# A recurrent and attention block on one core: the norm's statistics by transposing, one projection per sequence, shifted sequences rounded by VectorE

## The reference, cut to what matters

```python
def shift_token(t):
    t1, t2 = jnp.split(t, 2, axis=-1)
    t2 = jnp.pad(t2, ((0, 0), (1, 0), (0, 0)))[:, :-1]
    return jnp.concatenate([t1, t2], axis=-1)

def _layer(x, wqkv, qs, ksc, wo, lg, lb, w1, b1, w2, b2):
    h = shift_token(x)
    qkv = h @ wqkv
    ...
    x = x + o @ wo
    h = shift_token(x)
    mu = h.mean(-1, keepdims=True)
    var = h.var(-1, keepdims=True)
    h = (h - mu) / jnp.sqrt(var + 1e-05) * lg + lb
    h = h @ w1 + b1
    a, g = jnp.split(h, 2, axis=-1)
    h = a * jax.nn.gelu(g, approximate=False)
    return x + h @ w2 + b2
```

## Time and profile before

| | |
|---|---|
| median of 3 runs | 1315.2 us (1311.35 to 1317.98) |
| the profiled execution | 1315.54 us, its span 1313.7 us |
| busy PE, DVE, ACT, POOL | 96%, 83%, 88%, 87% of the span |
| attention, layer 0 and layer 1 | about 20 to 535 us, about 680 to 1196 us of the span |

### The profile page before, as it was taken

The page is one execution under the profiler, slowest core; times in us unless marked ns, Lnnn a source line. Parts: engine busy times, 40 slices in busy tenths (PEclk is TensorE's granted clock), DMA queues, the critical chain, the costliest instruction groups (busy, mean ns, idle before and its releaser), DMA issues.

```text
span 1313.7 us, 38163 instructions
## 1 busy us (share of the span) xinstructions
PE 1264.7 (96%) x13793; PEld 1011.5 (77%) x13794; DVE 1088.4 (83%) x1883; ACT 1162.1 (88%) x3529; POOL 1147.3 (87%) x840
## 2 busy tenths in 40 slices
PE   7889999999999999899988999999999999999998
PEld 4777888888888887566657788888888888876776
DVE  6788888888888887599877888899988898983777
ACT  4778999999999998787768899999999999998886
POOL 4888999999999998399778999999999999984776
PEclk9999999999999999999998999999999999999999
DMA  5122222222222221011011222221112222110223
GB/s 165 35 74 62 62 62 66 66 62 62 62 70 70 58 50 38 17 32 38 1 29 30 46 46 46 50 50 46 46 46 47 51 52 50 38 39 25 66 79 97
DMA packets 60298, 70.04 MB, mean 53 GB/s; under 512 B 8912, under 2 KB 38288, under 8 KB 60112
## 3 DMA queue, kind: packets, MB, share of 16 engines
q1 hardware_dynamic: 60112, 67.61, 20.5%
HBM read 13.33 MB, written 4.19 MB: 13 GB/s over the span
## 4 chain that ended last, share of the span: by engine, by line
PE 75%; POOL 7%; ACT 6%; DVE 5%; issue 4%; DMA 2%; SPq 1%; ACTq 0%; DVEq 0%; POOLq 0%
PE ps L203 59%; PE ps L268 8%; PE ps L278 3%; PE ps L281 3%; POOL t L1259 3%; ACT P L655 3%; POOL hxr L1259 2%; DVE t L975 1%; POOL P L1259 1%; DMA norm<-X 1%; DVE nm L1006 1%; DVE t L987 1%; ACT sqk L629 1%; DVE sums L994 1%; POOL side L1289 1%
## 5 line engine op out<-in xcount | busy, mean ns | idle before, releaser
L655 ACT ACTIVATE P<-ps,nm 128x128 f32<-128x128 f32 x1024 | 364.2, 384 | 4.2 <-DVE nm L1006 4.1
L203 PE MATMUL ps<-wqkv,hT 128*128 128x512 f32 x1152 | 330.7, 429 | 14.4 <-DVE t L975 10.4
L1259 POOL TENSOR_TENSOR t<-t 128x1024 f32<-128x1024 f32 x128 | 307.5, 2402 | 32.8 <-DVE t L975 30.4
L1259 POOL TENSOR_TENSOR P<-P,rden 128x512 f32<-128x512 f32 x256 | 294.6, 1160 | 31.0 <-DVE rden L1013 28.9
L203 PEld LDWEIGHTS ps<-wqkv,hT 128*128 128x128 f32 x1152 | 217.0, 190 | 92.0 <-issue 28.4
L1259 POOL TENSOR_TENSOR t<-t,rr 128x1024 f32<-128x1024 f32 x128 | 244.0, 1906 | 19.7 <-ACT rr L638 19.3
L655 ACT ACTIVATION_READ_ACCUMULATOR P<-ps,nm 128x1 f32 x1024 | 230.1, 225 | 0.0
L987 DVE TENSOR_TENSOR t<-ps,tabl 128x512 f32<-128x512 f32 x256 | 164.1, 683 | 41.0 <-ACT sqk L629 39.3
L1259 POOL TENSOR_TENSOR hxr<-hxf,hxr 128x512 fp32r<-128x512 f32 (+1 forms) x93 | 130.8, 1434 | 67.9 <-ACT hxr L711 67.8
L1006 DVE TENSOR_REDUCE nm<-ps 128x4 f32<-128x512 f32 x256 | 173.4, 679 | 6.4 <-PE ps L203 6.3
L645 ACT ACTIVATE PT<-ps 128x1024 f32<-128x1024 f32 x128 | 130.5, 1019 | 48.2 <-PE ps L268 47.3
(11 more groups left out here) (140 smaller groups left out, 2548.5 us busy)
## 6 DMA issues: line engine op xcount, KB each, us to landing
Vs<-Vn SPq DMA_DIRECT2D x224, 128.0 KB, 2.3
side<-in_x SPq DMA_DIRECT2D x17, 256.0 KB, 2.9
A<-X SPq DMA_DIRECT2D x16, 256.0 KB, 2.5
norm<-X SPq DMA_DIRECT2D x32, 128.0 KB, 2.2
norm<-X SPq DMA_DIRECT2D x32, 127.8 KB, 2.4
hsh<-X SPq DMA_DIRECT2D x31, 128.0 KB, 2.3
hsh<-X SPq DMA_DIRECT2D x31, 127.8 KB, 2.3
oT<-in_x SPq DMA_DIRECT2D x15, 256.0 KB, 2.9
```

The costliest lines, as they stand in the source:

```text
L203: return e.matmul(o, lhsT, rhs, start=start, stop=stop, skip_group_check=True)
L655: k = act(P[:, g, :], ps[:, 3 + s, (g % 4) * 128:(g % 4 + 1) * 128], ACT.Exp, bias=nm[:, g:g + 1], accum_out=den[:, g:g + 1])
L1259: return e.tensor_tensor(o, a, b_, op)
```

## The change

- `proj` is done once for a sequence, at r=3, with 512 columns in place of twice 256; `proj_add` likewise, at r=0.
- The mean and variance matmuls go. `turn_h` (r=0) transposes `h2` into bank 2 so that positions are on the partitions; VectorE takes statistics there (`stats_h`, r=1), ScalarE the root for four columns (`root_h`, r=1), VectorE applies both (`apply_h`, r=1), `turn_back` (r=2) transposes back and ScalarE copies to `B` (`keep_h`, r=3). `centre`, `scale_hc`, `square_hc`, `log_var` and `root_var` go.
- `shift_hi` is done by VectorE at r=2 for all but the first sequences; in layer 0 GpSimd's `shift_lo` moves from r=1 to r=3. `mv` has two buffers, and `ln_stats` moves from r=1 to r=0 in layer 0.
- The second feed-forward weight is split in two parts at steps `NT` and `NT` + 1 (ScalarE, then GpSimd in place of VectorE), before at steps 6 and 7; the decay constants (`set_decay`) at `NT` + 1 to `NT` + 3, before at steps 9 to 11.

```diff
-            def proj(l, b, u, bank):
+            def proj(l, b):
+                m = l * NB + b
+                e.wait_ge(s_o, l * NT + 4 * b + 4)
...
                 for c in range(4):
-                    k = mm(ps[:, bank, 0:256], wo[:, l, c, :], oT[:, c, u * 256:u * 256 + 256], c == 0, c == 3)
+                    k = mm(ps[:, 2, :], wo[:, l, c, :], oT[:, c, :], c == 0, c == 3)
                 k.then_inc(s_wo, 1)
 
-            def mean(l, b, bank):
-                e.wait_ge(s_h2, 32 * (l * NB + b + 1))
-                mm(ps[:, bank, :], avg, h2[:]).then_inc(s_mu, 1)
-
-            def var(l, b, bank):
-                e.wait_ge(s_sqh, l * NB + b + 1)
-                mm(ps[:, bank, :], avg, rsd[:]).then_inc(s_va, 1)
+            def turn_h(l, b):
+                m, bank = l * NB + b, turn_bank(l, b)
+                e.wait_ge(s_h2, 32 * (m + 1))
+                if l == 0 and b + 3 < NB:
+                    e.wait_ge(s_x, b + 4)
+                for t in range(TPB):
+                    k = e.transpose(ps[:, bank, t * 128:(t + 1) * 128], h2[:, t * 128:(t + 1) * 128], idf[:])
+                k.then_inc(s_nt, 1)
+
+            def turn_back(l, b):
+                m, bank = l * NB + b, back_bank(b)
+                e.wait_ge(s_na, m + 1)
+                if l and b + 1 < NB:
+                    e.wait_ge(s_osq, b + 2)
+                for t in range(TPB):
+                    k = e.transpose(ps[:, bank, t * 128:(t + 1) * 128], hn0[:, t * 128:(t + 1) * 128], idf[:])
+                k.then_inc(s_nu, 1)
...
-                    if (b := hit(i, 5)) is not None:
-                        e.wait_ge(s_o, l * NT + 4 * b + 2)
...
-                        proj(l, b, 0, 2)
                     if (b := hit(i, 7)) is not None:
...
-                        proj(l, b, 1, 2)
-                    if (b := hit(i, 8)) is not None:
-                        mean(l, b, 2)
+                        proj(l, b)
+                    if (b := hit(i, 8)) is not None and b < NB - 1:
+                        turn_h(l, b)
                     if (b := hit(i, 10)) is not None:
-                        var(l, b, 2)
+                        turn_back(l, b)
...
+            def root_h(l, b):
                 m = l * NB + b
...
+                e.wait_ge(s_ns, m + 1)
+                act(nrs, nmv[:, :, 1], ACT.Ln, bias=eps_ln).then_inc(s_nr0, 1)
+                e.wait_ge(s_nr0, m + 1)
+                act(nrs, nrs, ACT.Exp, scale=-0.5).then_inc(s_nr, 1)
+
+            def keep_h(l, b):
+                e.wait_ge(s_nu, l * NB + b + 1)
+                if l:
+                    e.wait_ge(s_hs, b + 1)
+                act(seq(B, b), ps[:, back_bank(b), :], ACT.Copy).then_inc(s_hn, 1)
...
+            def shift_hi(l, b):
+                m = l * NB + b
+                e.wait_ge(s_hsh, 32 * m)
+                e.wait_ge(s_vm, 4 * m - 4)
+                e.tensor_copy(hT[:, b % 2, 0, :], hsh[:, b % 2, :]).then_inc(s_hid, 1)
...
+            def stats_h(l, b):
+                m, x = l * NB + b, ps[:, turn_bank(l, b), :]
+                e.wait_ge(s_nt, m + 1)
+                for t in range(TPB):
+                    k = e.bn_stats(nst[:, t, :], x[:, t * 128:(t + 1) * 128])
+                k.then_inc(s_nb, 1)
+                e.wait_ge(s_nb, m + 1)
+                for t in range(TPB):
+                    k = e.bn_aggr(nmv[:, t, :], nst[:, t, :])
+                k.then_inc(s_ns, 1)
+
+            def apply_h(l, b):
+                m, x = l * NB + b, ps[:, turn_bank(l, b), :]
+                e.wait_ge(s_nr, m + 1)
                 if m:
...
+                    e.wait_ge(s_nu, m)
+                for t in range(TPB):
+                    k = ts(hn0[:, t * 128:(t + 1) * 128], x[:, t * 128:(t + 1) * 128], nmv[:, t, 0:1], nrs[:, t:t + 1],
+                           ALU.subtract, ALU.mult)
+                k.then_inc(s_na, 1)
```

More of the change, by code:

```diff
@@ L69, in program @@
         norm = sb("norm", [128, 3 * L])
-        h2, sq, rsd = (norm[:, j * L:(j + 1) * L] for j in range(3))
+        h2, hn0 = (norm[:, j * L:(j + 1) * L] for j in range(2))
         hsh = sb("hsh", [128, 2, L])
@@ L95, in program @@
         cw = [cols[:, 4 + j:5 + j] for j in range(4)]
-        one, eps_ln, eps_rms, ln2x8, mln2, part = (cst[:, i:i + 1] for i in range(6))
-        avg = part.to_broadcast([128, 128])
+        one, eps_ln, eps_rms, ln2x8, mln2 = (cst[:, i:i + 1] for i in range(5))
         ax, ez, u, dd, lnu, ru, half, nx, mx = (ab[:, i:i + 1] for i in range(9))
@@ L778, in scalar @@
                         norm_rt(l, i - 1)
+                    if (b := hit(i, 9)) is not None:
+                        root_h(l, b)
                     if i == 0:
@@ L853, in scalar @@
                     if b == 1:
-                        square_hc(l, NB - 1)
+                        e.preload_act_table_set(ATTN)
+                        root_h(l, NB - 1)
+                        e.preload_act_table_set(MIXED)
                     if b < NB:
@@ L1152, in vector @@
                     if (b := hit(i, 8)) is not None:
-                        proj_add(l, b, 1, 2)
-                    if l == 0:
-                        if (b := hit(i, 6)) is not None:
-                            proj_add(l, b, 0, 2)
-                        if (b := hit(i, 9)) is not None:
-                            centre(l, b, 2)
-                    else:
-                        if (b := hit(i, 13)) is not None:
-                            scale_hc(l, b)
+                        proj_add(l, b)
+                    if (b := hit(i, 9)) is not None:
+                        stats_h(l, b)
+                    if l:
                         for b in due(i, -2, {0: -1, 1: 5}):
@@ L1169, in vector @@
                         invert(l, i - 3, 1)
+                    if (b := hit(i, -2)) is not None and b >= 3 - l:
+                        shift_hi(l, b)
                     if l == 0:
-                        if (b := hit(i, 12)) is not None:
-                            scale_hc(l, b)
-                        for b in due(i, -7, {0: -1, 1: -1, 2: STATS[2]}):
+                        for b in due(i, -8, {0: -1, 1: -1, 2: STATS[2]}):
                             ln_stats(b)
@@ L1192, in vector @@
                         row_max(l, i - 2, 1)
-                    if l and (b := hit(i, 5)) is not None:
-                        proj_add(l, b, 0, 2)
                     if i == 1:
@@ L1201, in vector @@
                         row_max(l, 0, 1)
+                    if (b := hit(i, 9)) is not None:
+                        apply_h(l, b)
                     if l == 0 and i == STATS[1]:
@@ L1228, in vector @@
                             if b == 1 and j == 0:
-                                centre(l, NB - 1, 7)
+                                stats_h(l, NB - 1)
+                            if b == 1 and j == 1:
+                                apply_h(l, NB - 1)
                         if l == 0 and b == NB - 1:
```

223 lines of the change are left out of this document (89 added, 134 removed).

## The result

The changed kernel takes 1373.6 us (median of 4 runs, 1373.1 to 1374.7) where the kernel before took 1314.3 us beside it (4 runs, 1311.4 to 1318.0): a ratio of 1.0451, with a 95% interval of 1.0423 to 1.0479, so it is 59 us slower. The profiled execution has a span of 1372.8 us, against 1313.7.

What follows compares the result with a forecast made beforehand. TensorE and the other engines were taken as two side-by-side loops of equal length. Per sequence 1.4 us (layer 0) and 1.9 (layer 1), times 15, made 50; with 3 at the ends, 1315.5 became 1368 us, 8-in-10 range 1328 to 1388.

Steps and rivals of the forecast that it cites:

- r=3's `turn_qk` comes at most 0.37 us sooner in layer 0 and 0.15 in layer 1.: Steps r=0 to r=2: the other engines' chain stays, so TensorE's relief there wins at most these margins per sequence.
- Step r=3 gets 1.54 us longer, I take 1.6.: Attention step r=3: the half projection moved there from r=1 adds 1.6 us per sequence on TensorE.
- Layer 0: 1.4 us more for a sequence.: Layer 0's sum per sequence: 1.6 for r=3, less 0.37 margin, plus 0.2 for VectorE's `stats_h`.
- Layer 1: 1.9.: Layer 1's sum per sequence, in us more: 1.6 for r=3, less 0.15 margin, plus 0.45 for the cast.
- Its sign of being wrong: Wrong if a sequence takes 30.2 us with TensorE full, or new-norm waits (`turn_h`'s DMA, `turn_back` for `apply_h`) head TensorE's list.
- In layer 1 0.45 us is added in full: VectorE's cast `shift_hi` before r=2's rotation: 0.45 us per sequence in layer 1, nothing in layer 0 with its 0.38 gap.
- I set [weight split and decay constants] against each other at nothing, plus or minus 2 us.: Moving these small instructions from steps 6 to 11 to steps 64 to 67 changes nothing, within 2 us.
- GpSimd under 93 of 100 us in layer 0, TensorE near 95, waits for the rotation at the head: Expected mid-layer profile: these busy times; TensorE waiting at r=1 to r=3 for VectorE's rotation or ScalarE's `qT`.
- TensorE alone as the bound: Rival: TensorE alone sets the pace and its saving of 18 us arrives, 1297 us; chance 0.12.
- Absorbed in part: Rival: half of the 1.6 us projection block at r=3 comes back, 24 us less than forecast, 1344 us; chance 0.2.
- the prediction's main case: The forecast itself, 1368 us: r=3 pays 1.6 us, at most 0.37 or 0.15 comes back; chance 0.53.
- VectorE as the bound: Rival: VectorE's new work and a dearer cast in both layers add 22 us more, 1390 us; chance 0.1.

Runs made afterwards that it cites:

- e1: The kernel before with the output projection in one piece of 512 columns at r=3, its norm as it was: 1353.7 us, ratio 1.0269.
- e7: The kernel before with three of the four matmuls of the half projection at r=3 left out: 1310.2 us, ratio 0.9987.
- e11: The kernel before with the half projection of r=1 computed twice over: 1363.1 us, ratio 1.0343.
- e4: The changed kernel with GpSimd again rounding the shifted sequences (`shift_hi`) at its old places: 1370.1 us, ratio 1.0390.
- e5: The changed kernel with `apply_h` ahead of `norm_sum` on VectorE in layer 1: 1360.6 us, ratio 1.0321.
- e3: The changed kernel with the weight split (on VectorE) and decay constants back at steps 6 to 11: 1381.0 us, ratio 1.0526.
- e6: The kernel before with three of the four matmuls of the half projection at r=1 left out: 1307.1 us, ratio 0.9964.
- e9: e2 with `scale_hc` ahead of the reciprocal that releases GpSimd's second instruction: 1306.7 us, ratio 0.9955 to the kernel before.
- e2: The kernel before with only the second feed-forward weight and decay constants set late, in attention's last steps: 1312.8 us, ratio 0.9953.

## Why the prediction was right, and where it was not

The forecast of 1368 us lies 6 us under the measured 1374, and the sign and the main mechanism held. But it is that near by luck, since errors of both signs met. Its sum has, for the same stretches as above, 0, 14 x 1.4 = 19.6, 14 x 1.9 = 26.6, and 6.3 for the rest (two intervals and the ends); measured are -4.8, +14.1, +43.4 and +6.3. Layer 1 was priced 17 us too low, mostly for want of the wait for `apply_h`. Layer 0 was 5.5 us too high, because the forecast went by the steady 30.84 us while the first 14 sequences of before took 31.47 on average; and the 4.8 us at the start were not foreseen. The 6.3 of the rest agree by chance too: 3.3 of them are the gap in the feed-forward part.

- *"r=3's `turn_qk` comes at most 0.37 us sooner in layer 0 and 0.15 in layer 1."* This step held. In layer 0 the three steps take 22.78 us before and after. e1 shows it without the norm (+1.2 and +1.6 a sequence), and e7 shows that 0.1 us is all that a cut wins in layer 1.
- *"Step r=3 gets 1.54 us longer, I take 1.6."* It got 1.68 and 1.75 us longer. e11 gives the price of four matmuls of 256 columns more exactly: 1.73 us. Start to start of a half (1.54) was too low, as in the rows of e11 and before: 3.62 us busy for 16 entries, 1.89 for 8.
- *"Layer 0: 1.4 us more for a sequence."* The steady period grew by 1.67. The r=2 step has 7.64 us where it had 7.14: 0.23 for the rotation and 0.32 in front of the mask matmuls, because `keep_k` stands behind `apply_h`. That wait isn't in e1 and is in e4. The prediction had let nothing be lost there, by the gap of 0.38 us ahead of the rotation; `apply_h` itself, 1.36 us on VectorE, has no price in its sum.
- *"Layer 1: 1.9."* It grew by 3.24. The step of the sum that was too small is this one: it leaves out `rec_out`'s wait for `apply_h`, 15 times 1.65 = 24.8 us. It can't be subtracted whole (3.24 - 1.65 = 1.59), for e5 gives back 0.93 us a sequence when 1.35 of the wait goes. The prediction named `apply_h` only as something ahead of a rotation on VectorE, and listed `turn_back`, not `rec_out`, as the one that might wait for it. Its sign of being wrong, that a wait for the new `norm` tiles heads TensorE's list, came true in layer 1 (19.8 against 14.9 us), though not over the whole span. It didn't ask who writes bank 2 next, though the change made `rec_out` wait for that semaphore. e5 says that the place of `apply_h` in VectorE's order alone is worth 13 to 17 us.
- *"In layer 1 0.45 us is added in full"* for the cast, and nothing in layer 0. Its durations are 0.40 us in layer 1 and 0.83 in layer 0, so 0.45 was near; but e4 gives 0.23 and 0.1 us a sequence back. That the other half was covered by waits of the other engines is likely and wasn't tried.
- *"I set [weight split and decay constants] against each other at nothing, plus or minus 2 us."* This failed: e3 gives 7 to 10 us. In the kernel before they stood in VectorE's queue between the first rotations, and those first sequences were 5.3 and 1.5 us longer than the steady 30.84 (e3: 4.1 and 1.1 us of it are the constants'). The prediction priced the instructions in the steady state and never read the first sequences.
- *GpSimd under 93 of 100 us in layer 0, TensorE near 95, waits for the rotation at the head:* 88.1, 95.1 and 41.8 us. The waits for the rotation stand at r=1 and r=2, as forecast. In layer 1 TensorE's 91.1 is lower than foreseen, which is again `rec_out`, and a sequence takes 34.6 us where the forecast had 33.3.
- *The rivals.* TensorE alone as the bound falls with the change itself, which is slower, and with e6 and e7. Absorbed in part: in e1 0.52 us of layer 0's 1.54 came back, more than the prediction's main case allowed; in layer 1 next to nothing. VectorE as the bound: no, it fell to 84.2 of 100 us in layer 1.

What stays open: how much time another place of `apply_h` would win in r=2 of layer 0 and in the feed-forward part, since the two waits there are read from traces and no run takes them away; and the start of the kernel, where the reading of `mv` was not tried alone.

## What to carry to other kernels

Where several engines are within a few per cent of full, an engine without waits need not be a bound from which time can be taken: read how much later it is than what it would have waited for, and take that margin as the most that a cut wins, while what was added to a step here cost in full. Work that is collected from two steps into one can then lose on one side and gain next to nothing on the other. For each result that an edit leaves in a shared bank, ask who writes that bank next and where the last reader stands in its engine's order; for each instruction that it adds, ask what stands behind it there. When a profile shows a wait without a releaser, look in the program for what the instruction waits for, and compare ends and starts over several runs. And read the first sequences of a loop apart from its steady part, since constants set early are paid there.

## What the runs showed of the hardware

One VectorE instruction with two inputs in SBUF (128x512, `scale_hc`) took 0.66 us in e1, where it began while GpSimd was idle (GpSimd's own instruction then took 1.40 us in place of 1.03), 1.22 us in the kernel before, 1.32 in e9 with one GpSimd instruction beside it and 2.22 in e2 with two in a row. So it doesn't always get its turn between two instructions of GpSimd: in most sequences of before it did (it took 1.22 us, and GpSimd's two 2.49 in place of 2.04), in most of e2 it did not. What decides it, no run shows. The Trainium skill, "SBUF — State Buffer", section "Who interferes with whom", says that the later of the two waits for the whole of the other's instruction; the trace agrees for one and shows two. Sequences with the same instructions kept to one rhythm or the other by it (30.84 or 31.66 us): in layer 0 of before, e2, e6, e7 and e11 each sequence in which `scale_hc` took 2.2 us or more is one of the long ones, and in e9, where its place rules that out, no sequence after the first is above 31.34 us. The cast with one input in SBUF took 0.83 us beside GpSimd's `P` in layer 0 and 0.40 in layer 1, where it began ahead of GpSimd's, while `apply_h` out of PSUM took the same in both layers (404 ns for each 128x128):

```profile
L885 DVE TENSOR_SCALAR norm<-ps,norm 128x128 f32<-128x128 f32 x24 | 8.2, 404 | 0.0
L1006 DVE CAST hT<-hsh 128x512 fp32r<-128x512 f32 x6 | 5.0, 828 | 0.0
```

These are two groups of the changed kernel by line and shape, 200 to 400 us (count, busy us, mean ns of one, idle before).
